# A selective-scan image kernel: two delta chunks begin earlier in the schedule, and a depthwise convolution's matmuls skip the zero rim

## The chip, the cores and the metric

One core of a Trainium2 chip runs the whole program. The metric is the device time in microseconds (us) of one execution. The kernel before takes 4227.16 us, the median of three runs (4224.71 to 4227.22).

The engines are called as in the profile: PE (TensorE), DVE (VectorE), ACT (ScalarE), POOL (GpSimd), and SP, which issues the DMAs.

## What is computed

Sixteen images of 256 channels by 32 x 32 pass through two blocks, each with a residual addition. Cut to what matters:

```python
# block 0: a depthwise 7x7 convolution whose filters are computed from the image itself
x = x + conv7x7_depthwise(groupnorm(x), filters(groupnorm(x)), padding=3)
# block 1: three levels (32x32, 16x16, 8x8) of a two-way state-space scan, 16 states
f1 = 1x1 conv; f2 = 2x2 stride-2 conv of f1; f3 = 2x2 stride-2 conv of f2
delta = softplus(dt @ x + bias);  B, C = rows of x @ xw
for n in range(16):                       # states
    h[t] = exp(delta[t] * A[n]) * h[t-1] + delta[t] * B[n,t] * x[t]
    y[t] += C[n,t] * h[t]
out = (layernorm(y) of all levels, upsampled and added) * silu(z)
x = x + 1x1 conv(out)
```

## The kernel before: how the work is tiled and ordered

**Three images are in work at once.** `stages` (L1425) runs a body for the images i, j = i+1 and m = i+2. Each body is 37 units, numbered k = 0 to 36, and then a bridge. The scans of image i run in the units; so do the convolution of j and the filters of m. The first two bodies have no image i: body one prepares image 0, body two convolves it and prepares image 1. Then 14 bodies run in a hardware loop and two follow it. Every engine has its own `unit` and `bridge` function, written out by hand, and semaphores tie them.

**Units.** Unit 0 is the 8x8 level, all 16 states in both directions. Units 1 to 4 are the 16x16 level, four states each, in both directions. Units 5 to 20 are the 32x32 level forward, a state each, and 21 to 36 the same backward. For one unit

- SP fetches the broadcast rows B and C (`get_b`, `get_c`, L367) for unit k+2 while unit k runs,
- ACT writes exp(delta * A) into the PSUM tensor `slot_b` (`decay`, L1173),
- POOL multiplies B with u = delta * x into `bx` (`inputs`, L1315 and L1318),
- DVE scans (L552) and multiplies with C (`weigh`, L561; for unit 0 these are L525 and L531), in halves of 512 columns,
- POOL adds the products over the states and into y (`gather`, L1338 and L1343), one unit behind.

**Chunks.** Delta and u are made in six chunks: 0 and 1 for the two small levels, 2 and 3 for the two halves of the forward and 4 and 5 for those of the backward 32x32 level. A chunk passes PE (`chunk`, L831 and L832), ACT (`chunk_exp`, L1124 to L1133), DVE (`chunk_first`, L500), ACT (`chunk_log`, L1139), DVE (`chunk_last`, L508 and L510) and POOL (`chunk_low`, L1285 and L1287). SP stores the B and C rows to DRAM (`put_rows`, L360), from where they are fetched broadcast. The tables `CHUNK_PE`, `CHUNK_FIRST` and `CHUNK_LAST` say in which unit each step stands; PE's and ACT's steps of chunks 2 and 3 stand in units 0 and 1, the rest in units 1 and 2. `CHUNKS_OF` says which unit needs which chunks: unit 5 needs 2 and 3, unit 21 needs 4 and 5.

**Convolution.** `taps` (L777) runs the 98 taps (two halves of the channels, 49 taps each) as matmuls with a diagonal stationary matrix over a zero-padded image `pad` of 38 x 38. A tap is 6 matmuls of 512 columns: three products of high and low 16-bit parts, times two halves of 16 rows. `BRIDGE_TAPS` and `ROOM` set how many taps stand in each bridge and unit, `HALF_AT` the unit where DVE adds the first channel half into `xn` (`conv_add`, L486), and `row_unit` the unit where ACT makes each row of diagonal matrices (`make_row`, L1059; four rows of buffers).

**Bridge.** Here the scans of i end: norms 4 and 5, the product with silu(z), the output projection (L857), DVE's last addition (`output`, L628), the store of `ob` (L411). In between, chunks 0 and 1 of j are made, `project_z` (L807) runs, and ACT ends with the first decays of j, `y_start` (L1153, the first value of y), `keep_x` (L1079, a copy of `xn` to `xc`), the rest of the diagonals and `copy_x` (L1086, `xr` to `xn`). SP loads the image after next into `xr` (L394) once `copy_x` is done.

```python
def stages(unit, bridge, eng):
    def body(i, j, m):
        for k in range(NU):
            unit(i, j, m, k)
        bridge(i, j, m)
BRIDGE_TAPS = (0, 1, 3, 3, 3, 3, 6, 9)
CHUNK_PE = {0: 2, 1: 3, 13: 4, 14: 5}
CHUNK_FIRST = {1: 2, 2: 3, 14: 4, 15: 5}
CHUNK_LAST = {1: 2, 2: 3, 15: 4, 16: 5}
```

## Time and profile before

| | |
|---|---|
| median of the runs | 4227.16 us |
| the profiled execution: its own time | 4222.54 us |
| its span, first to last instruction | 4220.7 us |
| PE busy | 3109.9 us (74%), 12620 matmuls |
| DVE busy | 3209.0 us (76%) |
| ACT busy | 2693.2 us (64%) |
| POOL busy | 3290.3 us (78%) |
| mean granted TensorE clock | 0.873 of full speed |

The profile gives one execution. Its views used here are the page (shares, the chain that ended last), the groups of instructions by line, the timeline of an engine (start, duration, line, and in brackets how long the engine sat idle before and what ended that), and the table of stretches. A steady body of the loop lasts about 249 us; the one shown runs from 2005 to 2254 us. Body two, with the convolution of image 0, lies between about 70 and 256 us.

### The profile page before, as it was taken

The page shows a single profiled execution, that of the slowest core. Times are in us where ns is not written, and L with a number is a line of the kernel's source. Part 1 is how long each engine was busy: PE and PEld are TensorE (multiplying, and loading weights), DVE is VectorE, ACT ScalarE, POOL GpSimd, SP SyncE. Part 2 cuts the span into 40 slices and gives each one's busy share as a digit, 9 for nine tenths or more (in the row PEclk, how much of TensorE's full clock was granted, in tenths as well). Part 3 has the DMA queues.
Part 4 walks back from the last instruction along what each step waited for, and adds up shares of the span by engine and source line. Part 5 has one row for each costly group of instructions (what it writes and reads, how often), then busy time and mean ns, then how long its engine had stood idle before and what let it go on. Part 6 is the DMA issues. An engine that isn't in the chain of part 4 may idle for free.

```text
span 4220.7 us, 53011 instructions
## 1 busy us (share of the span) xinstructions
PE 3109.9 (74%) x12620; PEld 1400.2 (33%) x12620; DVE 3209.0 (76%) x3975; ACT 2693.2 (64%) x6662; POOL 3290.3 (78%) x1908
## 2 busy tenths in 40 slices
PE   6978777887777788777777877788787778877511
PEld 3433333333333333333333433333333333333200
DVE  1058788787877878787887878788787887878877
ACT  4467766666766666666656766665677666666532
POOL 0059698796968969697896969889696987969797
PEclk8989888998888899889898988999898889988755
DMA  1025455453545545354553544445354554635544
GB/s 41 1 101 195 147 163 169 157 205 127 186 150 166 186 136 204 134 178 152 170 201 122 199 149 165 161 168 203 119 195 145 167 170 157 204 118 192 163 165 167
DMA packets 187275, 664.08 MB, mean 157 GB/s; under 512 B 22736, under 2 KB 24672, under 8 KB 186976
## 3 DMA queue, kind: packets, MB, share of 16 engines
q1 hardware_dynamic: 186976, 661.47, 46.4%
q14 instruction: 280, 2.29, 0.2%
q8 instruction: 19, 0.31, 0.0%
HBM read 639.76 MB, written 21.63 MB: 157 GB/s over the span
## 4 chain that ended last, share of the span: by engine, by line
POOL 28%; issue 19%; ACT 16%; PE 14%; DVE 13%; DMA 7%; POOLq 1%; DVEq 1%; SPq 0%; ACTq 0%
POOL bx L1315 13%; POOL y L1343 7%; DMA bb<-bc_rows 7%; ACT diag L1059 7%; PE pconv L790 6%; POOL h L1338 5%; DVE h L561 4%; DVE slot_c L552 2%; POOL bx L1318 2%; DVE rs L508 2%; ACT slot_b L1173 2%; PE pm L832 1%; PE pm L807 1%; PE pm L831 1%; DVE rs L500 1%
## 5 line engine op out<-in xcount | busy, mean ns | idle before, releaser
L790 PE MATMUL pconv<-pad,diag 128*128 128x512 f16 x9408 | 2270.5, 398 | 314.3 <-ACT diag L1059 210.0
L790 PEld LDWEIGHTS pconv<-pad,diag 128*128 128x128 f16 x9408 | 932.0, 100 | 1618.0 <-issue 346.0
L1343 POOL TENSOR_TENSOR y<-y,h 128x1024 f32<-128x1024 f32 (+2 forms) x672 | 1324.5, 1971 | 162.9 <-DVE h L561 139.6
L1173 ACT ACTIVATE slot_b<-delta,nega 128x512 f32<-128x512 f32 (+1 forms) x1280 | 805.4, 639 | 951.3 <-DVE slot_c L552 911.6
L1315 POOL TENSOR_TENSOR bx<-bb,u 128x1024 f32<-128x1024 f32 x512 | 1220.1, 2383 | 31.9 <-DMA bb<-bc_rows 31.9
L552 DVE TENSOR_TENSOR_SCAN slot_c<-slot_b,bx 128x512 f32<-128x512 f32 (+1 forms) x1024 | 954.4, 956 | 315.6 <-POOL bx L1315 214.6
L561 DVE TENSOR_TENSOR h<-slot_c,cb 128x512 f32<-128x512 f32 x1280 | 860.6, 674 | 35.9 <-POOL y L1343 35.9
L552 DVE TENSOR_TENSOR_SCAN slot_c<-slot_b,slot_c,bx 128x512 f32<-128x512 f32 x512 | 663.6, 1296 | 74.5 <-ACT slot_b L1173 18.2
L1059 ACT ACTIVATE diag<-id,chi 128x128 f16<-128x128 f16 x1568 | 498.1, 387 | 10.3 <-PE pconv L790 9.6
L1059 ACT ACTIVATE diag<-id,clo 128x128 f16<-128x128 f16 x1568 | 496.4, 386 | 0.0
L1338 POOL TENSOR_TENSOR h<-h 128x512 f32<-128x512 f32 (+3 forms) x384 | 349.9, 911 | 20.9 <-DVE h L531 3.4
L1285 POOL TENSOR_TENSOR delta<-delta,rs 128x512 f32<-128x512 f32 (+1 forms) x96 | 97.7, 1017 | 324.6 <-DVE rs L510 324.6
L1318 POOL TENSOR_TENSOR bx<-bb,u 128x1024 f32<-128x1024 f32 x64 | 158.8, 2482 | 125.5 <-DMA bb<-bc_rows 97.9
L500 DVE SCALAR_TENSOR_TENSOR rs<-qs,es 128x512 f32<-128x512 f32 (+1 forms) x96 | 64.9, 676 | 223.6 <-ACT qs L1133 223.6
L831 PE MATMUL pm<-f,wbc 128*32 128x512 f32 (+1 forms) x192 | 102.3, 620 | 147.0 <-ACT delta L1129 74.2
L1295 POOL TENSOR_TENSOR f<-f,lnw 128x98 f32<-128x98 f32 x16 | 6.2, 388 | 182.8 <-ACT f L1003 182.8
L1139 ACT ACTIVATE qs<-qs 128x512 f32<-128x512 f32 (+1 forms) x96 | 50.5, 526 | 153.7 <-DVE rs L500 153.7
L852 PE MATMUL pm<-es,ones 128*128 128x512 f32 (+1 forms) x128 | 62.7, 573 | 113.2 <-ACT es L1183 113.2
L846 PE MATMUL pm<-y,cen 128*128 128x512 f32 (+1 forms) x128 | 60.3, 554 | 89.2 <-POOL y L1343 40.6
L722 PE MATMUL pm<-ident,xh 128*128 128x128 f32 x256 | 47.0, 343 | 98.3 <-ACT xg L1094 72.1
L832 PE MATMUL pm<-f,wdelta 128*128 128x512 f32 (+1 forms) x192 | 116.9, 698 | 0.0
L695 PE MATMUL pconv<-sg,grp 128*128 128x8 f32 x32 | 9.5, 371 | 145.5 <-DVE sg L431 145.5
(171 smaller groups left out, 3095.9 us busy)
## 6 DMA issues: line engine op xcount, KB each, us to landing
bb<-bc_rows SPq DMA_DIRECT2D x592, 512.0 KB, 4.4
cb<-bc_rows SPq DMA_DIRECT2D x592, 512.0 KB, 4.4
xr<-in_x SPq DMA_DIRECT2D x16, 1024.0 KB, 5.0
out<-ob SPq DMA_DIRECT2D x16, 1024.0 KB
bc_rows<-rows SPq DMA_DIRECT2D x64, 64.0 KB, 1.6
w<-in_w SPq DMA_DIRECT2D x2, 256.0 KB
wc<-in_wc SPq DMA_DIRECT2D x2, 256.0 KB
bc_rows<-rows SPq DMA_DIRECT2D x16, 32.0 KB, 4.0
```

The lines of the kernel that those rows point to most:

```text
L500: nc.vector.scalar_tensor_tensor(er[:, k, 0:n], qs[:, k, 0:n], 1.0, es[:, k, 0:n], ALU.subtract, ALU.subtract).then_inc(ch_err.sem, 1)
L552: ins = nc.vector.tensor_tensor_scan(hv, av, bv, start, ALU.mult, ALU.add)
L561: nc.vector.tensor_tensor(half(h[:, q % HR], b), bank(slot_c, b), half(cb[:, k % CR], b), ALU.mult).then_inc(q_pr.sem, 1)
L790: ins = nc.tensor.matmul(bank(pconv, k), w, pad[:, t, part, rows:rows + 16, dx:dx + W], start=first and m == 0, stop=last and m == 2)
L831: nc.tensor.matmul(bank(pm, 0)[0:2 * NS, 0:n], wbc[:, st, :], f[:, fc:fc + n], start=True, stop=True).then_inc(ch_bc.sem, 1)
L832: nc.tensor.matmul(bank(pm, 1)[:, 0:n], wdelta[:, st, :], f[:, fc:fc + n], start=True, stop=True).then_inc(ch_dt.sem, 1)
L1059: ins = nc.scalar.activation(diag[:, r % RING, m, dx, :], id16[:, :], ACT.Copy, scale=(chi, clo)[m][:, t, dy * KK + dx:dy * KK + dx + 1])
L1173: ins = nc.scalar.activation(slot_b[:, o:o + w], delta[:, so + c:so + c + w], ACT.Exp, scale=nega[:, st, n0 + n:n0 + n + 1])
L1315: ins = pool.tensor_tensor(bx[:, k % 2, :], bb[:, k % BR, :], us, ALU.mult)
L1318: ins = pool.tensor_tensor(o, bb[:, k % BR, :].rearrange("p (m l) -> p m l", m=m), us[:, None, :].to_broadcast([P, m, ln]), ALU.mult)
L1338: pool.tensor_tensor(src[:, 0:m], src[:, 0:m], src[:, m:2 * m], ALU.add).then_inc(n_y.sem, 1)
L1343: pool.tensor_tensor(yv, yv, src[:, 0] if len(src.shape) == 3 else src, ALU.add).then_inc(q_y.sem, 1)
```

## The change

`chunk` 2 of the next image moves from unit 0 into the end of the bridge on PE, and its `chunk_exp` on ACT there too, ahead of `y_start`. Chunk 3's move from unit 1 to unit 0. DVE's `chunk_first` of chunks 2 and 3 moves from behind the unit's products to between them (`CHUNK_MID`). `keep_x` and `copy_x` move from the bridge to unit 1, and the load into `xr` from unit 0 to unit 2. On SP the stores of the rows come behind the two fetches of their unit. One bridge tap fewer is taken, which by the tables moves row 4 of the diagonals from the bridge to units 1 and 2, and `HALF_AT` from unit 10 to unit 11. `inside` cuts a tap's matmul to the pixels whose source lies in the image; the first product of a channel half and its last keep the full size. Over a channel half the cut leaves 212 x 212 of 224 x 224 columns, and 0.898 of all with the full-size ones.

```diff
--- before.py
+++ after.py
@@ -383,13 +383,12 @@
 
             def unit(i, j, m, k):
                 if i is not None:
-                    for c, v in CHUNK_PE.items():
-                        if k == c + 1:
-                            put_rows(i, v)
                     if k + 2 < NU:
                         get_b(i, k + 2)
                         get_c(i, k + 2)
-                if k == 0 and j is not None and m is not None:
+                    if k in ROWS_OUT:
+                        put_rows(i, ROWS_OUT[k])
+                if k == 2 and j is not None and m is not None:
                     sp.wait_ge(a_copy.sem, a_copy.at(m, 0))
                     sp.dma_start(xr[:, :, :], xv[m]).then_inc(x_in.sem, 16)
 
@@ -568,6 +567,8 @@
                     return
                 late = halves_of(k - 1)[-1] if k > 1 else None
                 for q, p in halves_of(k):
+                    if k in CHUNK_MID and (q, p) == halves_of(k)[2]:
+                        chunk_first(i, CHUNK_MID[k])
                     same = late is not None and banks(late[0])[late[1]] == banks(q)[p]
                     if same:
                         weigh(i, *late)
@@ -786,8 +787,10 @@
                     dh, dl = diag[:, r % RING, 0, dx, :], diag[:, r % RING, 1, dx, :]
                     for m, (w, part) in enumerate(((dh, 0), (dh, 1), (dl, 0))):
                         for k in range(2):
-                            rows = dy + 16 * k
-                            ins = nc.tensor.matmul(bank(pconv, k), w, pad[:, t, part, rows:rows + 16, dx:dx + W],
+                            whole = (first and m == 0) or (last and m == 2)
+                            r0, r1, c0, c1 = inside(dy, dx, k, whole)
+                            ins = nc.tensor.matmul(img(bank(pconv, k), W)[:, r0:r1, c0:c1], w,
+                                                   pad[:, t, part, 16 * k + r0 + dy:16 * k + r1 + dy, c0 + dx:c1 + dx],
                                                    start=first and m == 0, stop=last and m == 2)
                     if dx == KK - 1:
                         ins.then_inc(row_done.sem, 1)
@@ -885,6 +888,8 @@
                     output(i, 0)
                     output(i, 1)
                 some(6, 7)
+                if j is not None:
+                    chunk(j, 2)
 
             pre = {5: lambda m: sums1(m, sa, pm, a_sums, a_stats), 6: lambda m: sums2(m, sa, pm, a_sums, a_spread),
                    15: a_key_, 16: lambda m: (a_turn(m, 0), a_turn(m, 1)), 17: lambda m: (a_turn(m, 2), a_turn(m, 3)),
@@ -1221,14 +1226,11 @@
                         act.wait_ge(ob_ready.sem, ob_ready.at(j, 0))
                     decay(j, 1, 0)
                     decay(j, 1, 1)
-                    y_start(j)
-                    keep_x(j)
                 if m is not None:
                     make_row(m, RING - 1, KK)
-                    for r in range(RING, NR):
-                        if row_unit(r) == 0:
-                            make_row(m, r)
-                    copy_x(m)
+                if j is not None:
+                    chunk_exp(j, 2)
+                    y_start(j)
 
             pre = {6: a_mean_, 7: a_rstd_, 8: a_xh_, 16: a_keyb_, 17: lambda m: (a_xtc_(m, 0), a_xtc_(m, 1)),
                    18: lambda m: (a_xtc_(m, 2), a_xtc_(m, 3), a_exp_(m)),
@@ -1258,6 +1260,11 @@
                 if i is not None:
                     if k in CHUNK_PE:
                         chunk_exp(i, CHUNK_PE[k])
+                    if k == 1:
+                        keep_x(i)
+                if j is not None and k == 1:
+                    copy_x(j)
+                if i is not None:
                     if k == 5:
                         silu_exp(i)
                     if k == 6:
@@ -1374,13 +1381,15 @@
 
 TAPS = NR * KK
 PREP = NU - 4
-BRIDGE_TAPS = (0, 1, 3, 3, 3, 3, 6, 9)
+BRIDGE_TAPS = (0, 1, 3, 3, 3, 3, 6, 8)
 FIRST_TAPS = 2
 
 
 
-CHUNK_PE = {0: 2, 1: 3, 13: 4, 14: 5}
-CHUNK_FIRST = {1: 2, 2: 3, 14: 4, 15: 5}
+CHUNK_PE = {0: 3, 13: 4, 14: 5}
+ROWS_OUT = {0: 2, 1: 3, 14: 4, 15: 5}
+CHUNK_MID = {1: 2, 2: 3}
+CHUNK_FIRST = {14: 4, 15: 5}
 CHUNK_LAST = {1: 2, 2: 3, 15: 4, 16: 5}
 
 ROOM = [49 if k < 5 else 27 for k in range(NU)]
@@ -1396,6 +1405,14 @@
 
 
 HALF_AT = next(k for k in range(NU) if taps_at(k + 1) > TAPS // CT)
+
+
+def inside(dy, dx, k, whole):
+
+    if whole:
+        return 0, 16, 0, W
+    reach = KK // 2
+    return (max(reach - dy - 16 * k, 0), min(H + reach - dy - 16 * k, 16), max(reach - dx, 0), min(W + reach - dx, W))
 
 
 def row_unit(r):
```

**DVE, units 0 to 1 of the first body that scans** (`h` is the weighed product, `slot_c` the scan, `rs` the chunk's buffer er). Before:

```order
L561 TENSOR_TENSOR h<-slot_c,cb 128x512
L542 REGISTER_ALU
L552 SCALAR_TENSOR_TENSOR slot_c<-slot_b,bx 128x256 x2
L558 REGISTER_ALU
L560 ISA
L561 TENSOR_TENSOR h<-slot_c,cb 128x512
L497 ISA
L499 REGISTER_ALU
L500 SCALAR_TENSOR_TENSOR rs<-qs,es 128x512
L508 TENSOR_TENSOR rs<-qs,rs 128x512
L510 TENSOR_TENSOR rs<-rs,es 128x512
```

And now:

```order
L499 SCALAR_TENSOR_TENSOR rs<-qs,es 128x512
L541 ISA
L551 SCALAR_TENSOR_TENSOR slot_c<-slot_b,bx 128x256 x2
L557 REGISTER_ALU
L560 TENSOR_TENSOR h<-slot_c,cb 128x512
L541 REGISTER_ALU
L551 SCALAR_TENSOR_TENSOR slot_c<-slot_b,bx 128x256 x2
L557 REGISTER_ALU
L559 ISA
L560 TENSOR_TENSOR h<-slot_c,cb 128x512
L507 TENSOR_TENSOR rs<-qs,rs 128x512
L509 TENSOR_TENSOR rs<-rs,es 128x512
```

The first pass of chunk 2 (L500, now L499) has moved ahead of two of the unit's four scans; the last two passes stand where they stood.

**ACT, the end of the bridge** (`a` and `slot_b` are decays, `y` is `y_start`, `xc` is `keep_x`, `xn` is `copy_x`, `rows` begins a chunk). Before:

```order
L1173 ACTIVATE slot_b<-delta,nega 128x256 x4
L1153 ACTIVATE y<-f,vec 128x1024
L1153 ACTIVATE y<-f,vec 128x256
L1153 ACTIVATE y<-f,vec 128x64
L1153 ACTIVATE y<-f,vec 128x1280
L1153 ACTIVATE y<-f,vec 128x64
L1079 ACTIVATE xc<-xn 128x2048
L1059 ACTIVATE diag<-id,clo 128x128 x7
L1054 REGISTER_ALU
L1059 ACTIVATE diag<-id,chi 128x128 x7
L1059 ACTIVATE diag<-id,clo 128x128 x7
L1086 ACTIVATE xn<-xr 128x2048
```

And now:

```order
L1178 ACTIVATE slot_b<-delta,nega 128x256 x4
L1064 ACTIVATE diag<-id,clo 128x128 x7
L1126 REGISTER_ALU
L1128 ISA
L1129 ACTIVATE rows<-pm 32x512
L1133 ACTIVATE es<-pm,vec 128x512
L1134 ACTIVATE delta<-pm,vec 128x512
L1136 ACTIVATE es<-es 128x512
L1138 ACTIVATE qs<-es 128x512
L1158 ACTIVATE y<-f,vec 128x1024
```

Chunk 2 stands between seven diagonals and `y_start`; 14 diagonals and both copies have left the bridge.

**PE, units 13 and 14 of the loop** (`pm<-f` are the chunks 4 and 5, `pconv` the taps). Before:

```order
L825 REGISTER_ALU
L831 MATMUL pm<-f,wbc 32x512
L832 MATMUL pm<-f,wdelta 128x512
L790 MATMUL pconv<-pad,diag 128x512 x6
L777 REGISTER_ALU
L790 MATMUL pconv<-pad,diag 128x512 x6
L829 REGISTER_ALU
L831 MATMUL pm<-f,wbc 32x512
L832 MATMUL pm<-f,wdelta 128x512
```

And now:

```order
L828 REGISTER_ALU
L834 MATMUL pm<-f,wbc 32x512
L835 MATMUL pm<-f,wdelta 128x512
L792 MATMUL pconv<-pad,diag 128x13x29
L792 MATMUL pconv<-pad,diag 128x16x29
L792 MATMUL pconv<-pad,diag 128x13x29
L792 MATMUL pconv<-pad,diag 128x16x29
L792 MATMUL pconv<-pad,diag 128x13x29
L792 MATMUL pconv<-pad,diag 128x16x29
L832 REGISTER_ALU
L834 MATMUL pm<-f,wbc 32x512
L835 MATMUL pm<-f,wdelta 128x512
```

Between the two chunks stands one tap, where two stood.

## Rows read from the trace of the kernel before

**Rows 1.** The page: busy shares, and the chain that ended last

```profile
PE 3109.9 (74%) x12620; PEld 1400.2 (33%) x12620; DVE 3209.0 (76%) x3975; ACT 2693.2 (64%) x6662; POOL 3290.3 (78%) x1908
POOL 28%; issue 19%; ACT 16%; PE 14%; DVE 13%; DMA 7%; POOLq 1%; DVEq 1%; SPq 0%; ACTq 0%
```

**Rows 2.** Timeline of POOL, head of a body: start, us, operation [idle before]

```profile
2013.18 2.36 POOL L1318 TENSOR_TENSOR bx<-bb,u 128x1024 f32<-128x1024 f32 x1 [7.08 <-DMA bb<-bc_rows]
2015.49 2.94 POOL L1338 TENSOR_TENSOR h<-h 128x512 f32<-128x512 f32 x4
...
2021.88 0.32 POOL L1343 TENSOR_TENSOR y<-y,h 128x64 f32<-128x64 f32 x1 [0.16 <-POOL h L1338]
2025.58 1.27 POOL L1285 TENSOR_TENSOR delta<-delta,rs 128x512 f32<-128x512 f32 x1 [3.38 <-DVE rs L510]
...
2037.87 1.27 POOL L1285 TENSOR_TENSOR delta<-delta,rs 128x512 f32<-128x512 f32 x1 [0.69 <-DVE rs L510]
```

**Rows 3.** Timeline of DVE, the same stretch

```profile
2001.74 1.61 DVE L628 SCALAR_TENSOR_TENSOR ob<-slot_b,vec,xc 128x512 f32<-128x512 f32 x2 [1.72 <-PE slot_b L857]
...
2022.63 0.69 DVE L500 SCALAR_TENSOR_TENSOR rs<-qs,es 128x512 f32<-128x512 f32 x1 [2.96 <-ACT qs L1133]
2024.02 0.69 DVE L508 TENSOR_TENSOR rs<-qs,rs 128x512 f32<-128x512 f32 x1 [0.69 <-ACT qs L1139]
2024.74 0.69 DVE L510 TENSOR_TENSOR rs<-rs,es 128x512 f32<-128x512 f32 x1
...
2036.63 1.10 DVE L510 TENSOR_TENSOR rs<-rs,es 128x512 f32<-128x512 f32 x1
```

**Rows 4.** Timeline of ACT, the same stretch

```profile
2005.10 1.67 ACT L1173 ACTIVATE slot_b<-delta,nega 128x256 f32<-128x256 f32 x4 [2.74 <-DVE ob L628]
2006.71 3.27 ACT L1153 ACTIVATE y<-f,vec 128x1024 f32<-128x1024 f32 x5
...
2011.68 2.14 ACT L1059 ACTIVATE diag<-id,clo 128x128 f16<-128x128 f16 x7
...
2019.61 0.57 ACT L1124 ACTIVATE rows<-pm 32x512 f32<-32x512 f32 x1
...
2021.87 0.63 ACT L1133 ACTIVATE qs<-es 128x512 f32<-128x512 f32 x1
...
2053.82 0.69 ACT L1173 ACTIVATE slot_b<-delta,nega 128x512 f32<-128x512 f32 x1 [8.31 <-DVE slot_c L552]
```

**Rows 5.** Timeline of PE, bridge, end of the bridge and unit 1

```profile
1993.20 4.21 PE L790 MATMUL pconv<-pad,diag 128*128 128x512 f16 x18
...
2009.47 1.05 PE L831 MATMUL pm<-f,wbc 128*32 128x512 f32 x2
...
2021.47 1.88 PE L831 MATMUL pm<-f,wbc 128*32 128x512 f32 x2 [4.54 <-ACT delta L1129]
```

**Rows 6.** Timeline of DVE, units 14 to 16

```profile
2115.09 0.69 DVE L500 SCALAR_TENSOR_TENSOR rs<-qs,es 128x512 f32<-128x512 f32 x1 [1.16 <-ACT qs L1133]
...
2120.75 1.97 DVE L508 TENSOR_TENSOR rs<-qs,rs 128x512 f32<-128x512 f32 x1
2122.75 2.72 DVE L510 TENSOR_TENSOR rs<-rs,es 128x512 f32<-128x512 f32 x1
```

**Rows 7.** Timeline of POOL, units 14 and 15

```profile
2110.35 2.35 POOL L1315 TENSOR_TENSOR bx<-bb,u 128x1024 f32<-128x1024 f32 x1 [1.51 <-DMA bb<-bc_rows]
...
2117.25 1.27 POOL L1285 TENSOR_TENSOR delta<-delta,rs 128x512 f32<-128x512 f32 x1 [2.23 <-DVE rs L510]
```

**Rows 8.** Timeline of PE, units 10 to 14

```profile
2090.50 1.47 PE L790 MATMUL pconv<-pad,diag 128*128 128x512 f16 x6 [1.87 <-DVE xn L486]
...
2106.63 3.91 PE L790 MATMUL pconv<-pad,diag 128*128 128x512 f16 x12
```

**Rows 9.** Timeline of PE, body two

```profile
70.56 49.99 PE L790 MATMUL pconv<-pad,diag 128*128 128x512 f16 x216 [10.52 <-ACT diag L1059]
```

**Rows 10.** Timeline of DVE, body two

```profile
138.42 1.28 DVE L486 SCALAR_TENSOR_TENSOR xn<-pconv,csc,xn 128x1024 f32<-128x1024 f32 x1 [43.00 <-PE pconv L790]
```

## The prediction, made before the changed kernel ran

> **What bounds the kernel now.** I read the page first. No engine is busy all the time: POOL 78%, DVE 76%, PE 74%, ACT 64%, and the chain that ended last runs over POOL, ACT, PE and DVE in turn [rows 1]. So no single total sets the time. What counts is which wait ends last in each stage, and for that I went through the timelines of one steady body, 2005 to 2254 us, engine by engine.
>
> POOL works without a gap for most of a body. Its gaps lie at three places: the bridge, the head of the body, and units 14 to 16. In the head it waits 7.08 us for a transfer, then 3.38 us and 0.69 us for DVE's last pass of chunks 2 and 3 [rows 2]. DVE made chunk 2 late because its first pass waited 2.96 us for ACT and its second another 0.69 us [rows 3]. And ACT came to chunk 2 late, at 2019.61 us, since `y_start`, 21 diagonals and two copies stood ahead of it [rows 4]. PE had the chunk's first matmul issued at 2009.47 us [rows 5]. So in the head the bound is a queue on ACT, then the chain ACT, DVE, POOL.
>
> The convolution does not bound a steady body: DVE waits for it nowhere there, and where PE and the addition of the first channel half meet it is PE that waits, 1.87 us [rows 8]. It binds only in body two, where DVE sat idle 43.00 us until PE had done the first half of the taps [rows 10].
>
> **The head: chunks 2 and 3 start earlier.** On ACT, before, the decays began at 2005.10 us and took 1.67 us [rows 4]. Now seven diagonals of 2.14 us follow, then chunk 2, which took 2022.50 - 2019.61 = 2.89 us, so it is done at about 2011.7 us instead of 2022.5. DVE's first pass then waits for nothing. DVE's unit 1 still ends where it did (2019.68 us, 2022.63 less the wait of 2.96), plus the pass of 0.69 us, then two more passes of 0.69: 2021.7 us. POOL is through with the sums of unit 0 at 2021.88 + 0.32 = 2022.2 us [rows 2]. The wait of 3.38 us is gone, and so is the 0.69 us of chunk 3. Together 4.07 us.
>
> Against this, the passes now run while POOL works, where before POOL stood idle. A pass beside POOL took 1.10 us in unit 2 instead of 0.69 [rows 3]. The last two of chunk 2 lie on the path, so I take 0.8 us off: 3.25 us for each of 16 images, **52 us**. The bounds are 4.07 x 16 = 65 us, and 1.7 x 16 = 27 us where half is lost.
>
> What else moves there costs nothing, and this is the cover. The copies and 21 diagonals took ACT from 2009.98 to 2019.61 us; seven diagonals of 2.1 us stay, and 7.5 us go to units 1 and 2. ACT has room behind them: it later sat idle 8.31 us at once [rows 4]. Without that cover the decays of unit 3 would be late. On SP the load into `xr` now stands behind the fetches of unit 4 and a unit later; DVE reads `xr` at the end of unit 3, a further unit of 12 us on (chunk 2's step to chunk 3's, 2025.58 to 2037.87 us [rows 2]). The stores of rows 2 and 3 come behind two fetches but their sources are ready earlier, and no fetch but that of unit 5 waits for them. `y_start` is late next: it ends at 2011.7 + 3.27 = 2015.0 us, and POOL wants it at 2015.49 us [rows 2, 4]. The wait of 7.08 us for the transfer of unit 2 stays, since that fetch is issued behind the store of `ob`.
>
> **The bridge: three taps ahead of the output projection.** 18 matmuls take 4.21 us [rows 5], `project_z` and the output follow in PE's order, and DVE waits 1.72 us for the output [rows 3]. These taps keep 29 of 32 rows and 31 of 32 columns on average, 0.88, which saves 0.5 us. It shifts DVE's last addition, the store and all that follows. 15 bridges with both images: **7 us**; bounds 0 and 8.
>
> **Units 13 to 16: chunks 4 and 5.** Between chunk 4 and chunk 5 PE ran 12 tap matmuls in 3.91 us [rows 8], and one tap of the two is now behind chunk 5. That makes chunk 5 ready some 2 us earlier, and DVE's wait for it is 1.16 us [rows 6]; POOL's next step waits for DVE [rows 7]. So at most 1.16 us. The other way, the addition of the first channel half moves from unit 10 to 11, so PE meets it with a longer gap, and the spread of norm 1 comes behind two taps that may run at the lower clock. After a gap of 4.54 us the chunk's first matmul took 1.88 us instead of 1.05, nearly twice as long, as at the lower of the clock's two levels, 1.2 and 2.4 GHz [rows 5]. I take 1.0 us, 15 bodies: **15 us**; bounds 0 and 17.
>
> In unit 14 the fetch of B no longer stands behind the row store, so POOL's wait of 1.51 us for it goes [rows 7]. I cost it at nothing, as POOL waits for DVE 2.23 us a few steps later and simply waits longer; were that cover gone too, it would be worth up to 24 us.
>
> **Body two.** Its 588 tap matmuls take 49.99 / 216 = 0.231 us each [rows 9], 136 us, and PE is the bound there. Keeping 0.898 of the columns saves up to 13.9 us. Some of it is fixed cost per matmul: **13 us**; bounds 0 (if a matmul's time did not go by columns) and 14. In the 14 loop bodies the rest of the saving, about 13 us each, lies beside other work: PE waits for diagonals afterwards.
>
> **Sum.** 52 + 7 + 15 + 13 = 87 us. Against the profiled execution's own 4222.5 us that is 4135.5; the median of the runs stands 4.6 us above it, so I forecast **4140 us**, 2.1% faster.
>
> **The rivals.**
>
> *`y_start` is late.* The margin above is 0.5 us. It stands behind chunk 2 on ACT, and chunk 2 on PE stands behind DVE's clip of z. If PE's two matmuls take 1.88 us each, as at the lower clock [rows 5], ACT ends `y_start` at 2016.5 or later, and POOL's sums start 1 to 1.5 us later. 1.4 x 16 = 22 us less: 4162 us. For it: the margin. Against it: PE is busy right before. 18%.
>
> *The middle gives nothing.* PE meets the addition in unit 11 after a gap, its taps run at the lower clock, norm 1 and with it chunk 4 come later by what chunk 5 gains. 4155 us, or 4170 with a loss of 1 us per body. 12%.
>
> *The cut saves PE no time.* A matmul over rows of 29 to 31 pixels may take what a full one takes. Then the 7 and 13 us are not there: 4160 us. No row shows a trimmed matmul. 7%.
>
> *More is had:* the 1.51 us of unit 14 and the whole 4.07 us count. 87 + 24 + 13 = 124 us, 4103 us. 10%.
>
> *The other side: DVE's passes stretch beside POOL.* In unit 16 two passes next to POOL's long additions took 1.97 and 2.72 us instead of 0.69 [rows 6]. If all six passes of chunks 2 and 3 cost 2.72 us, that is 6 x 2.03 = 12.2 us more per body on DVE. The waits removed are 2.96 + 0.69 for chunk 2 [rows 3] and 0.69 for chunk 3 [rows 2], 4.3 us. The rest, 7.9 x 16 = 126 us, less the 35 us of the other terms, gives 4318 us. It decides once a pass costs on average more than 0.69 + 4.3 / 6 = 1.4 us. Against it: in the head POOL's operations are the short sums of units 0 to 2, four in 2.94 us [rows 2], and a pass beside them took 1.10 us [rows 3]. 5%.
> The Trainium skill (SBUF — State Buffer, the part on contention) speaks against the change here: a VectorE instruction with two SBUF inputs and a GpSimd instruction exclude each other for the whole instruction, and the loser is blocked. By that rule a pass would wait for the rest of whichever POOL operation runs, up to a whole addition; the rows of 2.72 us agree, and those of 1.10 us agree too, as the POOL operations there are short.
>
> *No change that can be measured.* The waits only move to POOL's next transfer or to the bridge. POOL has no gap between the head and unit 14, which speaks against it. 6%.
>
> **How the numbers follow.** The forecast has 42%, the rivals 18, 12, 7, 10, 5 and 6%. The range runs from the case with more to be had, 4100 us, to 4187 us, which takes in the late `y_start` together with an empty middle or with no saving from the cut; the bounds of the head alone give 4127 to 4165. It leaves out the slow side and no change. Within 0.2% of the time before, about what a measurement of this kernel can tell from no change, I put 6%; faster 0.88, slower 0.06.
>
> **What would show it.** In the profile after: POOL's waits for L510 in units 1 and 2 (3.38 and 0.69 us) near nothing, DVE's wait for ACT before its first pass of chunk 2 gone, that pass at about 1 us. `y_start` ending before POOL's first sum; if not, POOL's first L1338 shows a wait for ACT. Tap matmuls at about 0.21 us when dense. DVE's wait of 1.16 us in unit 15 gone. Body two shorter by 13 us, a loop body by 4 to 5 us out of 249. It would be wrong if POOL showed a new gap between units 3 and 13, or DVE passes in units 1 and 2 above 1.4 us.

## The result, and the profile after

| | before | after |
|---|---|---|
| median of the runs shown together | 4225.93 us (4 runs) | 4173.91 us (4 runs) |
| ratio, 95% interval | | 0.9879 [0.9864, 0.9895] |
| span of the profiled execution | 4220.7 us | 4171.0 us |
| first store of `ob` (bodies one to three) | at 506.17 us | at 495.31 us |
| mean of the 13 loop bodies that follow | 249.46 us | 246.71 us |
| last two bodies | 467.2 us | 464.1 us |

The change is 52 us faster, 1.2%, where 87 us were forecast. The spans differ by 49.7 us: 10.9 before the first store, 13 x 2.75 = 35.7 in the loop, 3.1 at the end.

First the busy times on the page of the kernel after, beside [rows 1], and two of its groups of instructions (busy, mean ns of one, then idle before them):

```profile
PE 2972.9 (71%) x12620; PEld 1412.1 (34%) x12620; DVE 3275.1 (79%) x3975; ACT 2698.8 (65%) x6662; POOL 3307.2 (79%) x1908
...
L1292 POOL TENSOR_TENSOR delta<-delta,rs 128x512 f32<-128x512 f32 (+1 forms) x96 | 97.6, 1017 | 272.0 <-DVE rs L509 272.0
L499 DVE SCALAR_TENSOR_TENSOR rs<-qs,es 128x512 f32<-128x512 f32 (+1 forms) x96 | 123.3, 1285 | 167.0 <-ACT qs L1138 167.0
```

The last of these groups in the kernel before:

```profile
L500 DVE SCALAR_TENSOR_TENSOR rs<-qs,es 128x512 f32<-128x512 f32 (+1 forms) x96 | 64.9, 676 | 223.6 <-ACT qs L1133 223.6
```

PE lost 137 us of work. DVE gained 66 us and POOL 17, though both do exactly what they did before. That is the first sign: something makes the same instructions longer. The first pass of a chunk (`chunk_first`, L499) takes 1285 ns in the mean where it took 676; that alone is 58 us of DVE's 66.

The head of a body, whose store of `ob` is at 1977.19 us. POOL's timeline after, beside [rows 2] (that body's store is at 2005.24 us):

```profile
1984.37 2.96 POOL L1325 TENSOR_TENSOR bx<-bb,u 128x1024 f32<-128x1024 f32 x1 [5.91 <-DMA bb<-bc_rows]
1987.30 3.27 POOL L1345 TENSOR_TENSOR h<-h 128x512 f32<-128x512 f32 x4
...
1990.92 3.61 POOL L1345 TENSOR_TENSOR h<-h 128x512 f32<-128x512 f32 x4
...
1994.98 1.27 POOL L1292 TENSOR_TENSOR delta<-delta,rs 128x512 f32<-128x512 f32 x1
...
2006.75 1.27 POOL L1292 TENSOR_TENSOR delta<-delta,rs 128x512 f32<-128x512 f32 x1
```

The low part of chunk 2 (L1292) no longer waits for DVE. It starts 17.8 us behind the store; before it was 20.3. That of chunk 3 has lost its wait of 0.69 us too. The head is now held by the landing of `bb` and POOL's own chain. That chain got longer: the sums of 2.94 us take 3.27 and 3.61, and `bx` 2.96 in place of 2.36.

ACT's timeline of the same head, beside [rows 4]:

```profile
1980.70 0.57 ACT L1129 ACTIVATE rows<-pm 32x512 f32<-32x512 f32 x1
...
1983.50 3.26 ACT L1158 ACTIVATE y<-f,vec 128x1024 f32<-128x1024 f32 x5
```

Chunk 2 is on ACT 3.5 us behind the store in place of 14.4. `y_start` ends at 1986.8, half a microsecond ahead of POOL's first sum.

Units 14 to 16, DVE's timeline, beside [rows 6]:

```profile
2078.01 2.55 DVE L499 SCALAR_TENSOR_TENSOR rs<-qs,es 128x512 f32<-128x512 f32 x1 [1.40 <-ACT qs L1138]
...
2084.20 1.14 DVE L499 SCALAR_TENSOR_TENSOR rs<-qs,es 128x512 f32<-128x512 f32 x1
2085.26 0.68 DVE L507 TENSOR_TENSOR rs<-qs,rs 128x512 f32<-128x512 f32 x1
2085.97 0.69 DVE L509 TENSOR_TENSOR rs<-rs,es 128x512 f32<-128x512 f32 x1
```

and POOL's, beside [rows 7]:

```profile
2077.64 2.37 POOL L1322 TENSOR_TENSOR bx<-bb,u 128x1024 f32<-128x1024 f32 x1
2082.44 2.35 POOL L1350 TENSOR_TENSOR y<-y,h 128x1024 f32<-128x1024 f32 x1 [2.43 <-DVE h L560]
2086.81 1.26 POOL L1292 TENSOR_TENSOR delta<-delta,rs 128x512 f32<-128x512 f32 x1 [2.02 <-DVE rs L509]
```

POOL's wait for the fetch, 1.51 us, is gone, as is DVE's 1.16 us ahead of chunk 5's pass. But chunk 4's first pass takes 2.55 us in place of 0.69.

Body two, the taps on PE and the addition of the first channel half on DVE, beside [rows 9, 10]:

```profile
70.68 46.77 PE L792 MATMUL pconv<-pad,diag 128*128 128x512 f16 x216 [10.52 <-ACT diag L1064]
```
```profile
133.65 1.28 DVE L485 SCALAR_TENSOR_TENSOR xn<-pconv,csc,xn 128x1024 f32<-128x1024 f32 x1 [40.34 <-PE pconv L792]
...
209.46 1.28 DVE L485 SCALAR_TENSOR_TENSOR xn<-pconv,csc,xn 128x1024 f32<-128x1024 f32 x1 [19.44 <-PE pconv L792]
```

A tap matmul takes 216.5 ns in the mean of this stretch where it took 231.4. In both kernels the granted clock is 0.50 until about 74 us, where the first ten or so matmuls lie. The rest run at the full clock, at about 211 ns after and 222 before. The second addition was at 219.09 us, so it comes 9.6 us earlier, not 13.

### The profile page after: what moved, and what is told of

It is laid out like the page before. It is cut to its first block, busy times and chain, and to the rows that moved or that the text cites. A ratio compares the mean times of both kernels' runs of the same rounds, so it can differ in the third digit from the quotient of the medians.

```text
span 4171.0 us, 53040 instructions
## 1 busy us (share of the span) xinstructions
PE 2972.9 (71%) x12620; PEld 1412.1 (34%) x12620; DVE 3275.1 (79%) x3975; ACT 2698.8 (65%) x6662; POOL 3307.2 (79%) x1908
## 4 chain that ended last, share of the span: by engine, by line
issue 21%; DVE 20%; POOL 19%; ACT 18%; PE 15%; DMA 6%; DVEq 1%; POOLq 0%; SPq 0%; ACTq 0%
ACT diag L1064 9%; POOL bx L1322 9%; PE pconv L792 8%; DVE h L560 7%; DVE slot_c L551 7%; POOL y L1350 6%; DMA bb<-bc_rows 6%; ACT slot_b L1178 3%; POOL h L1345 2%; DVE rs L507 1%; PE pm L810 1%; POOL bx L1325 1%; DVE xn L485 1%; PE pm L835 1%; PE pm L834 1%
## 5 line engine op out<-in xcount | busy, mean ns | idle before, releaser
L792 PE MATMUL pconv<-pad,diag 128*128 128x464 f16 (+11 forms) x9408 | 2142.0, 385 | 439.4 <-ACT diag L1064 304.1
L792 PEld LDWEIGHTS pconv<-pad,diag 128*128 128x128 f16 x9408 | 942.2, 102 | 1609.7 <-issue 362.8
L560 DVE TENSOR_TENSOR h<-slot_c,cb 128x512 f32<-128x512 f32 x1280 | 860.2, 673 | 23.7 <-POOL y L1350 23.7
L1345 POOL TENSOR_TENSOR h<-h 128x512 f32<-128x512 f32 (+3 forms) x384 | 365.9, 953 | 22.6 <-ACT y L1158 3.9
L1292 POOL TENSOR_TENSOR delta<-delta,rs 128x512 f32<-128x512 f32 (+1 forms) x96 | 97.6, 1017 | 272.0 <-DVE rs L509 272.0
L499 DVE SCALAR_TENSOR_TENSOR rs<-qs,es 128x512 f32<-128x512 f32 (+1 forms) x96 | 123.3, 1285 | 167.0 <-ACT qs L1138 167.0
L849 PE MATMUL pm<-y,cen 128*128 128x512 f32 (+1 forms) x128 | 70.4, 636 | 123.6 <-POOL y L1350 49.1
L723 PE MATMUL pm<-ident,xh 128*128 128x128 f32 x256 | 56.9, 396 | 137.8 <-ACT xg L1099 70.4
L834 PE MATMUL pm<-f,wbc 128*32 128x512 f32 (+1 forms) x192 | 84.0, 520 | 37.4 <-ACT delta L1134 19.9
L1294 POOL TENSOR_TENSOR u<-delta,f 128x512 f32<-128x512 f32 (+1 forms) x96 | 97.8, 1018 | 7.5
L723 PEld LDWEIGHTS pm<-ident,xh 128*128 128x128 f32 x256 | 45.1, 204 | 155.6 <-ACT xg L1099 80.2
```

Source lines behind the costliest of these rows:

```text
L499: nc.vector.scalar_tensor_tensor(er[:, k, 0:n], qs[:, k, 0:n], 1.0, es[:, k, 0:n], ALU.subtract, ALU.subtract).then_inc(ch_err.sem, 1)
L560: nc.vector.tensor_tensor(half(h[:, q % HR], b), bank(slot_c, b), half(cb[:, k % CR], b), ALU.mult).then_inc(q_pr.sem, 1)
L723: ins = nc.tensor.transpose(bank(pm, g % 2)[:, (2 * b + t) * P:(2 * b + t + 1) * P], xh[:, t, n * P:(n + 1) * P], ident[:, :])
L792: ins = nc.tensor.matmul(img(bank(pconv, k), W)[:, r0:r1, c0:c1], w, pad[:, t, part, 16 * k + r0 + dy:16 * k + r1 + dy, c0 + dx:c1 + dx], ...
L834: nc.tensor.matmul(bank(pm, 0)[0:2 * NS, 0:n], wbc[:, st, :], f[:, fc:fc + n], start=True, stop=True).then_inc(ch_bc.sem, 1)
L1345: pool.tensor_tensor(src[:, 0:m], src[:, 0:m], src[:, m:2 * m], ALU.add).then_inc(n_y.sem, 1)
```

## Landmarks for the experiments

The same four points of a body tell where each kernel gains. They are starts on POOL, in us behind the store of `ob` that opens the body, as means over the twelve middle bodies: the low parts of chunks 2, 3 and 4, and the low half of the weights (`wlo`); then the next store. Three more columns count bodies of those twelve. "Held" bodies have chunk 2's low part 0.9 us or more later than the kernel's best body; they are split by what is seen in them. In those held by products, DVE's two products of unit 0 take 4.4 to 4.5 us instead of 2.33. In those held by `bb`, the products take 2.33 us and POOL's `bx` behind them starts only 8.3 us or more behind the store, when `bb` has landed. "Slow PE" has the two centring matmul groups of the bridge at 1.3 to 2.0 us instead of 1.08 and 1.02.

| kernel | chunk 2 | chunk 3 | chunk 4 | `wlo` | next store | held by products | held by `bb` | slow PE |
|---|---|---|---|---|---|---|---|---|
| before | 20.34 | 32.63 | 112.60 | 175.24 | 249.44 | 0 | 0 | 1 |
| after | 18.17 | 29.95 | 110.01 | 172.64 | 246.54 | 4 | 0 | 2 |
| e1 no cut | 17.61 | 29.40 | 109.50 | 172.18 | 246.65 | 0 | 0 | 3 |
| e2 cut only | 20.34 | 32.62 | 111.77 | 174.61 | 248.37 | 0 | 0 | 1 |
| e3 store first | 18.33 | 30.12 | 109.50 | 172.15 | 245.80 | 1 | 4 | 0 |
| e4 half at 10 | 17.84 | 29.62 | 109.68 | 172.30 | 246.06 | 0 | 0 | 1 |
| e5 first passes behind | 18.33 | 30.64 | 110.70 | 173.31 | 247.65 | 3 | 1 | 5 |
| e6 rows only | 17.93 | 29.70 | 109.75 | 172.36 | 246.34 | 2 | 0 | 2 |
| e7 columns only | 17.65 | 29.43 | 109.51 | 172.14 | 246.28 | 0 | 1 | 1 |
| e8 store and turn | 17.87 | 29.65 | 107.84 | 170.79 | 245.79 | 1 | 0 | 10 |
| e9 bridge tap | 19.68 | 31.46 | 110.36 | 173.32 | 245.70 | 8 | 0 | 0 |
| e10 turn, no cut | 17.71 | 29.49 | 108.87 | 171.83 | 246.04 | 0 | 1 | 1 |
| e11 changed again | 18.37 | 30.15 | 110.20 | 172.83 | 246.60 | 2 | 3 | 1 |
| e12 POOL waits | 20.27 | 32.05 | 110.45 | 173.40 | 245.77 | 0 | 0 | 0 |

From chunk 3 to chunk 4 the kernel before took 79.97 us, the one after 80.06: the middle lost a tenth where 1.0 us was forecast to be gained. From `wlo` to the next store it was 74.20 and is 73.90. In bodies without slow PE matmuls it is 74.05 us before, 74.07 in e1 and 73.62 after; a slow body takes 1.6 us more.

## The experiments

All twelve kernels compute the whole result. They were run in groups of four (e1 to e4), four (e5 to e8), three (e9 to e11) and one (e12), each beside the kernel before on the same chip, whose medians there were 4219.2, 4223.8, 4223.0 and 4222.3 us. So ratios are compared, and times within a group.

**The two halves of the change.** e1 is the change without the cut:

```
-                            whole = (first and m == 0) or (last and m == 2)
+                            whole = True
```

> The changed kernel with every tap's matmul at its full 512 columns (same result, no cut). Theory: the cut is worth 10 us in body two and 0.45 us per bridge (15 bridges, 7 us), and nothing elsewhere, as PE waits for diagonals or DVE in a steady body. Expected 4174 + 17 = 4191 us (4186 to 4196); a loop body 0.5 us longer than the 246.7 us of the changed kernel. Rival: the cut takes cover away in the middle of a body (PE meets the addition of the first half after a gap, at the lower clock), so that without it a loop body is shorter: 4165 to 4180 us.

Measured: 4179.7 us, ratio 0.9901 [0.9886, 0.9916]. By the ratios that is 9 us above the changed kernel, not the 17 expected, and a loop body is 0.1 us longer, not 0.5. The rival's range holds the time, but its shorter loop body isn't there. e2 puts the cut alone into the kernel before.

> The kernel before with the cut alone. Theory: 10 us in body two and 7 us in the bridges, nothing else: 4226 - 17 = 4209 us (4203 to 4214), a loop body of 249.0 us against 249.5. Rival: the taps between chunks 4 and 5 lie on the path too (two taps, 0.4 us per body), then 4202 us.

Measured: 4200.97 us, ratio 0.9953 [0.9939, 0.9966]. In the changed order the cut is worth about 10 us ahead of the first store (505.22 against 495.31 us) and nothing in a loop body (246.65 against 246.54 us). That nothing is a difference: the stretch from `wlo` to the next store is 0.6 us shorter, and chunk 2's low part comes 0.6 us later behind the store (17.61 against 18.17). In the old order the cut is worth 1.1 us a body, where 0.5 was expected: chunk 4 comes 0.8 us earlier by it, as the rival had it, and the stretch behind `wlo` is 0.4 us shorter. So in the loop the two parts don't add up. By the ratios the order alone is worth 42 us and the cut alone 20, together 51 to 56 (e11); with intervals of 6 us each way those totals alone would not show it.

**The middle.** e3 restores the old place of the store of rows in SP's order for units 14 and 15:

```
+                    if k in ROWS_OUT and k > 1:
+                        put_rows(i, ROWS_OUT[k])
                     if k + 2 < NU:
                         get_b(i, k + 2)
                         get_c(i, k + 2)
-                    if k in ROWS_OUT:
+                    if k in ROWS_OUT and k < 2:
                         put_rows(i, ROWS_OUT[k])
```

> The changed kernel with SP's stores of chunk rows 4 and 5 again ahead of the two fetches of units 14 and 15; those of chunks 2 and 3 stay behind. Theory: the wait of POOL for that fetch (1.51 us before, 0 after) was cover. With it POOL stands idle while DVE makes its first pass of chunk 4, which took 0.69 us before and 2.55 us after, beside a POOL operation of 2.37 us. With the store first again: POOL waits about 1.5 us for the fetch, the pass takes 0.7 us, the last step of chunk 4 on POOL comes 1.8 us earlier, a loop body is about 245.0 us, and the kernel 4174 - 27 = 4147 us (4140 to 4155). Rival: the middle lost time since the addition of the first half moved to unit 11 (PE at the lower clock there); then this changes nothing or costs the 1.5 us: 4172 to 4197 us.

Measured: 4158.3 us, ratio 0.9852 [0.9836, 0.9867]; the next store at 245.80 us, chunk 3 to chunk 4 in 79.38 us. The gain is less than half of the 27 us expected, but the rival's "nothing" falls. DVE's timeline of units 14 and 15, and POOL's:

```profile
2070.14 0.69 DVE L501 SCALAR_TENSOR_TENSOR rs<-qs,es 128x512 f32<-128x512 f32 x1 [1.32 <-ACT qs L1140]
...
2074.63 2.48 DVE L501 SCALAR_TENSOR_TENSOR rs<-qs,es 128x512 f32<-128x512 f32 x1
```
```profile
2071.89 2.36 POOL L1324 TENSOR_TENSOR bx<-bb,u 128x1024 f32<-128x1024 f32 x1 [1.95 <-DMA bb<-bc_rows]
2074.21 2.35 POOL L1352 TENSOR_TENSOR y<-y,h 128x1024 f32<-128x1024 f32 x1
```

With POOL made to wait 1.95 us for its fetch again, chunk 4's pass falls into that gap and takes 0.69 us. The next pass, 1.14 us after the change, now meets POOL's `y` and ends at 2077.1 us, half a microsecond behind it. So 1.9 us were gained and 1.3 lost, and the low part of chunk 4 comes 0.7 us earlier from chunk 3 on. The kernel before shows what the wait had been worth, DVE and POOL:

```profile
2109.35 0.69 DVE L500 SCALAR_TENSOR_TENSOR rs<-qs,es 128x512 f32<-128x512 f32 x1 [1.14 <-ACT qs L1133]
```
```profile
2106.44 2.40 POOL L1343 TENSOR_TENSOR y<-y,h 128x1024 f32<-128x1024 f32 x1
2110.35 2.35 POOL L1315 TENSOR_TENSOR bx<-bb,u 128x1024 f32<-128x1024 f32 x1 [1.51 <-DMA bb<-bc_rows]
```

There the same pass lay between two of POOL's operations. After the change it starts at 2078.01 us while POOL is at work until 2080.01, and ends at 2080.56, as if it had begun only when POOL was through. So does e3's second pass.
The Trainium skill (SBUF — State Buffer, the part on contention) states this: a VectorE instruction with two SBUF inputs and a GpSimd instruction that reads SBUF exclude each other for a whole instruction. The trace agrees, and also where an instruction doesn't have two such inputs: DVE's product L560, one of whose inputs is in PSUM, keeps 673 ns in the mean over 1280 of them in the kernel after, though POOL is busy 79% of the time.

e4 tests the rival, that the addition of the first channel half costs the middle its gain by having moved from unit 10 to 11:

```
-HALF_AT = next(k for k in range(NU) if taps_at(k + 1) > TAPS // CT)
+HALF_AT = 10
```

> The changed kernel with DVE's addition of the first channel half back in unit 10. Theory (the pass beside POOL): no effect within 0.2%, 4166 to 4182 us, as ACT waited only 1.05 us for the spread of norm 1 and DVE did not wait for norm 1. Rival (the addition in unit 11 is what cost the middle its gain): 1 to 1.8 us less per body, 4147 to 4160 us.

Measured: 4165.3 us, ratio 0.9872 [0.9857, 0.9888], from chunk 3 to 4 in 80.06 us as after. No effect on the middle. The mean body is 0.5 us shorter, but that lies in the head, where none of the twelve bodies happened to be held.

**The head.** e5 puts the first passes of chunks 2 and 3 behind the products again:

```
-CHUNK_MID = {1: 2, 2: 3}
-CHUNK_FIRST = {14: 4, 15: 5}
+CHUNK_MID = {}
+CHUNK_FIRST = {1: 2, 2: 3, 14: 4, 15: 5}
```

> The changed kernel, but VectorE's first passes of chunks 2 and 3 stand behind the products of units 1 and 2 again instead of between them; everything else as changed. Theory A (placement matters a little: in the changed kernel the head is now held by POOL's own chain from the landing of bb, 2.96 + 3.27 + 3.61 us, so a later pass first eats slack of about 0.5 us and then costs): low part of chunk 2 starts 0.3 to 1.5 us later behind the out store than the changed kernel's 18.01 us, chunk 3 likewise, time 4178 to 4200 us (ratio to the kernel before 0.989 to 0.994). Rival B (the placement is most of the head's gain, 2.3 us a body): chunk 2's low part back at 20 us or more, time 4208 to 4215 us. Rival C (the pass between the products only stretches POOL's sums, 3.27 and 3.61 us against 2.94 before, so that behind them is better): low part at 17.0 to 17.5 us, time 4160 to 4170 us.

Measured: 4188.2 us, ratio 0.9912 [0.9899, 0.9926]. In bodies that aren't held chunk 2's low part is at 17.7 to 17.9 us as after, and chunk 3's at 30.0 to 30.2 against 29.5 to 29.8, since DVE's second pass waits 0.70 us for ACT again. In bodies held by the products chunk 2's low part is 1.9 us late, where after the change it is 1.0. B and C fall. Theory A's time and cost hold, but not its place: chunk 2 in a body that isn't held comes no later. The passes between the products bring 0.3 to 0.4%, part of it by the clock in the bridge (slow in five of twelve bodies of e5). Most of the head's gain is ACT's order, which e5 has too.

**The cut.** e6 leaves out rows only, e7 columns only. By symmetry each leaves out 12 of 224 lines of the seven shifts, the same number of columns of PE's work.

```
-    return (max(reach - dy - 16 * k, 0), min(H + reach - dy - 16 * k, 16), max(reach - dx, 0), min(W + reach - dx, W))
+    return max(reach - dy - 16 * k, 0), min(H + reach - dy - 16 * k, 16), 0, W
```

> The changed kernel, with the tap products cut only in whole image rows (all 32 columns kept). Mean columns per matmul 485 of 512. Theory A (columns cost 0.417 ns each at the full clock, and what the full cut loses, about 5 ns per matmul, is the broken rows of 29 to 31 columns): the tap matmul in body two takes 231 - 11 = 220 ns, body two is 6 us shorter than with no cut (full cut: 9.6), ratio to the kernel before 0.9886. Rival B (the 5 ns are a fixed cost of any matmul on a window that is not the whole bank): 225 ns, 3 us shorter, ratio 0.9893.

> The changed kernel, with the tap products cut only in columns (all 16 rows kept, rows of 29 to 32). Mean columns per matmul again 485 of 512. Theory A (broken rows cost about 5 ns more): the tap matmul in body two takes 225 to 226 ns, body two 3 to 3.5 us shorter than with no cut, ratio 0.9893. Rival B (fixed cost for any cut window): the same 225 ns as with rows alone. Rival C (no extra cost of either alone): 220 ns both, and the two savings would then add up to more than the full cut's 15 ns.

The first stretch of taps in body two, of e1, e6 and e7 in turn:

```profile
70.39 49.96 PE L792 MATMUL pconv<-pad,diag 128*128 128x512 f16 x216 [10.52 <-ACT diag L1064]
```
```profile
67.93 48.34 PE L792 MATMUL pconv<-pad,diag 128*128 128x512 f16 x216 [10.52 <-ACT diag L1064]
```
```profile
70.91 49.01 PE L792 MATMUL pconv<-pad,diag 128*128 128x512 f16 x216 [10.52 <-ACT diag L1064]
```

| | ns per matmul, first stretch | from the first tap to the second addition, us | saved, us |
|---|---|---|---|
| nothing cut (e1) | 231.3 | 148.51 | |
| rows only (e6) | 223.8 | 142.22 | 6.29 |
| columns only (e7) | 226.9 | 145.61 | 2.90 |
| both (after) | 216.5 | 138.78 | 9.73 |

Rows save twice what columns save, for the same number of columns streamed. Per matmul of all 588 that is 10.7 and 4.9 ns. The rates of the first stretch show less of a difference, since its 36 of 49 taps hold only 51 of the 84 lines that the row cut leaves out. An estimate of what there was to save: each of the two leaves out 15,744 columns, which at the 222 ns that 512 columns take at the full clock are worth 6.8 us. Rows save nearly that, columns less than half. The totals, 4170.7 us, 0.9873 [0.9857, 0.9888] and 4172.6 us, 0.9879 [0.9864, 0.9894], can't be told from the change's own, as expected of 3 to 7 us. Theory A holds in the trace, and rival B, that rows and columns save alike, falls: a matmul whose rows are broken to 29 to 31 pixels costs more than its columns. Why it does wasn't taken apart.

**On from e3.** e8 also turns the order in unit 15, so that chunk 4's last passes go ahead of chunk 5's first:

```
+                    if k in CHUNK_LAST:
+                        chunk_last(i, CHUNK_LAST[k])
                     if k in CHUNK_FIRST:
                         chunk_first(i, CHUNK_FIRST[k])
-                    if k in CHUNK_LAST:
-                        chunk_last(i, CHUNK_LAST[k])
```

> The changed kernel with two edits for the middle: the store of rows goes out ahead of the fetches in units 14 and 15 (as in e3_store_first), and in unit 15 VectorE does the two last passes of chunk 4 ahead of the first pass of chunk 5. Theory A (a VectorE pass that meets a POOL operation on SBUF lasts until that operation ends): one pass, the first of the last two of chunk 4, still meets POOL's y of 2.35 us and takes about 2.5 us, the other 0.69; POOL's low part of chunk 4 starts about 0.7 us earlier than in e3_store_first (which had it at 109.72 us behind the out store), chunk 5's first pass then meets POOL's low part of chunk 4 and takes 1 to 1.5 us; time 4145 to 4160 us, ratio 0.982 to 0.986. Rival B (what chunk 4 gains, chunk 5 gives back, since its logarithm comes later): chunk 4's low part 0.7 us earlier, chunk 5's at 118.08 us as in e3, time 4156 to 4162 us, ratio 0.985 to 0.9865.

Measured: 4158.0 us, ratio 0.9843 [0.983, 0.9857]. Both expected ranges hold that time. Chunk 4 does come 1.7 us earlier than in e3, 107.84 us, and chunk 5 some 1.3 us earlier, so rival B falls; `wlo` is 1.4 us earlier; and the next store is where it was, 245.79 against 245.80. The gain went in the bridge. PE's timeline there and the granted clock (table of stretches: length, busy PE, PE's loads, DVE, ACT, POOL, then the clock), e8:

```profile
2198.09 1.65 PE L851 MATMUL slot_b<-y,cen 128*128 128x512 f32 x2
2199.53 1.91 PE L851 MATMUL slot_c<-y,cen 128*128 128x512 f32 x2
```
```profile
2185.00:2190.00 5.00, 5.00 (x10) 1.98 (x9) 3.40 (x4) 5.00 (x16) 2.04 (x2) 0.68 0.00 0
2190.00:2195.00 5.00, 3.92 (x19) 2.33 (x18) 0.89 (x2) 5.00 (x16) 2.73 (x2) 1.00 0.00 0
2195.00:2200.00 5.00, 3.91 (x17) 2.30 (x16) 0.23 (x1) 2.70 (x11) 0.00 (x0) 0.85 0.01 2
2200.00:2205.00 5.00, 5.00 (x13) 1.63 (x12) 0.45 (x2) 3.57 (x9) 2.10 (x3) 0.81 0.61 216
```

and e3:

```profile
2198.59 1.08 PE L851 MATMUL slot_b<-y,cen 128*128 128x512 f32 x2
2199.50 1.02 PE L851 MATMUL slot_c<-y,cen 128*128 128x512 f32 x2
```
```profile
2195.00:2200.00 5.00, 3.91 (x21) 2.42 (x19) 0.23 (x1) 3.23 (x12) 0.00 (x0) 1.00 0.01 2
2200.00:2205.00 5.00, 5.00 (x19) 2.17 (x18) 0.85 (x3) 4.57 (x11) 1.65 (x3) 1.00 0.62 216
```

In e8 the clock falls from the upper level, 2.4 GHz, to the lower, 1.2, for part of these stretches, after PE had come back to the upper one by 2190. Ahead of all this PE had idled 4.96 us, in e3 as in e8. Ten of twelve bodies show it, and those are 1.6 us longer between `wlo` and the store. e9 puts one tap more into the bridge, between the two projections, where PE idled 1.08 us:

```
-BRIDGE_TAPS = (0, 1, 3, 3, 3, 3, 6, 8)
+BRIDGE_TAPS = (0, 1, 3, 4, 4, 4, 6, 8)
```

> e8_store_and_turn, with one tap more (6 products) in the bridge between the projection onto f and its lower levels, where TensorE idled 1.1 us in e8 (2.2 us in e3), and one tap less behind. Why: in e8 ten of the twelve middle bodies show the two centring matmuls of the bridge at 1.41 to 1.79 and 1.91 us, in e3 none does (1.08 and 1.02 us), and each of the ten is 1.6 us longer between the start of the low half of the weights and the next out store; the granted clock of the 5 us around them is 0.81 to 0.85 in e8 and 1.00 in e3. Theory A (the clock fell after the idle stretches around the projection, and a filled one keeps it): centring matmuls at 1.08 and 1.02 us in most bodies, mean body 244.2 to 244.8 us, time 4135 to 4145 us, ratio 0.9795 to 0.982. Rival B (the fall depends on where the stage lies, not on this gap): nothing changes in the matmuls, the tap delays the lower levels by 0.2 to 0.5 us, mean body 246 us, time 4156 to 4165 us, ratio 0.984 to 0.9865.

Measured: 4152.8 us, ratio 0.9833 [0.982, 0.9846]. e10 is e8 with nothing cut:

> e8_store_and_turn with all tap products whole (nothing cut). Theory A (the shorter tap products leave TensorE more idle, so its clock falls more often in the bridge, and the cut takes there what it gives elsewhere): fewer than 5 of 12 bodies with slow centring matmuls against 10 of 12 in e8, mean body 244.5 to 245.3 us, body two and its neighbours 9 to 10 us longer, time 4148 to 4158 us. Rival B (the fall comes from the stage being earlier, whatever the taps take): 8 or more of 12 bodies with slow ones, mean body 245.8 us or more, time 4165 to 4172 us, ratio 0.9865 to 0.988.

Measured: 4176.3 us, ratio 0.9892 [0.9877, 0.9907], a mean body of 246.0 us. Both take the falls away (0 and 1 of 12). In both PE has more work ahead of that place than in e8. But e3 kept the clock with more idle time there (2.22 us), so the gap alone doesn't decide, and what does stays open. Neither reached the time expected of it. In e10 whole taps bring chunk 4 a microsecond later than in e8. In e9 `wlo` to the next store is 72.4 us in place of 75.0, but the next head takes back 1.8, for a reason given below.

**What holds the head.** e11 is the changed kernel again, in one group with e9 and e10.

> The changed kernel as it is, beside the two others on one chip, to set the variants' gains against it. Both theories: ratio 0.988 (0.9864 to 0.9895 before). Theory A (VectorE's second product of unit 0 and POOL's first bx of the body block each other whenever bx starts ahead of it): again some of the twelve middle bodies, 3 to 7, show POOL's low part of chunk 2 at 18.8 to 19.0 us behind the out store and the product at twice its length (4.50 against 2.33 us for two), and the rest 17.8 us; a body is 1.0 to 1.2 us longer for it. Rival B (that difference is one of the DMA's landing alone): products at 2.33 us in both kinds of body.

Measured: 4169.7 us, ratio 0.9868 [0.9853, 0.9883]; five of twelve bodies held. In two of the five the products take 4.5 us, as theory A has it. In the other three they take 2.33 us, and `bx` starts only 8.7 to 9.2 us behind the store, as rival B has it. So there are two ways to be held, and neither theory covers both. In the first profile after, all four held bodies are of the first kind; in e3 four of five are of the second. Why `bb` lands later in some bodies wasn't looked into.

The first kind. Two bodies of the first profile after, DVE's timeline, the one held first:

```profile
2968.36 4.50 DVE L530 TENSOR_TENSOR h<-cb,h 128x1024 f32<-128x1024 f32 x2
...
3215.17 2.33 DVE L530 TENSOR_TENSOR h<-cb,h 128x1024 f32<-128x1024 f32 x2
```

and POOL's:

```profile
2969.18 2.59 POOL L1325 TENSOR_TENSOR bx<-bb,u 128x1024 f32<-128x1024 f32 x1 [5.14 <-DMA bb<-bc_rows]
...
3216.49 3.23 POOL L1325 TENSOR_TENSOR bx<-bb,u 128x1024 f32<-128x1024 f32 x1 [5.64 <-DMA bb<-bc_rows]
```

In the first, `bb` lands 0.8 us into the products of the least level (L530). POOL's `bx` goes ahead of the second product, which ends only after it: 4.50 us for two. In the second, `bx` starts 1.3 us into them and is itself the one that stands, 3.23 us for 2.36. What decides is whether `bx` or the second product starts first. Here that is a few tenths of a microsecond of a transfer's landing, 6.7 or 6.9 us behind the store, and the held body is 1.0 to 1.2 us longer. Here it is the body in which `bb` lands earlier that is held.

Why the kernel before has no such body among the twelve, though `bb` lands as early there: its second product starts 6.49 us behind the store, and `bx` never ahead of 6.57. After the change the second product starts at 6.68 to 6.97. The scan ahead of it became longer, and it is the cut that did this, not the order. POOL's `bx` of unit 1 and DVE's scan of unit 0, in e1 (store at 1986.39 us) and after (1977.19 us):

```profile
1984.96 2.36 POOL L1325 TENSOR_TENSOR bx<-bb,u 128x1024 f32<-128x1024 f32 x1 [2.13 <-issue]
1987.32 4.53 DVE L524 TENSOR_TENSOR_SCAN h<-a,b 128x1040 f32<-128x1040 f32 x2
```
```profile
1976.11 2.35 POOL L1325 TENSOR_TENSOR bx<-bb,u 128x1024 f32<-128x1024 f32 x1 [2.04 <-issue]
1978.12 4.74 DVE L524 TENSOR_TENSOR_SCAN h<-a,b 128x1040 f32<-128x1040 f32 x2
```

The cut brings the store forward by 0.45 us, but this `bx` hardly comes forward with it. It ended as the scan began, 0.93 us behind the store; now it ends 0.3 us into the scan, and the scan loses 0.2 us, in other bodies up to 0.47. With nothing cut (e1, e10) the scan takes 4.53 us and no body is held by the products. With the cut in the old order (e2) the second product takes 3.4 us in five of the twelve bodies, at no cost, since chunk 2 waits for ACT there. In e9, whose bridge is shorter still, `bx` of unit 1 lies wholly beside the scan, which takes 5.9 to 6.1 us, and eight bodies are held: that is the 1.8 us.

e12 makes POOL wait, in e9:

```
+                    if k == 0:
+                        pool.wait_ge(q_pr.sem, q_pr.at(i, 2))
                     if k + 1 < NU:
                         inputs(i, k + 1)
```

> e9_bridge_tap with one wait more: in unit 0 POOL holds its first operation (bx of unit 1) until VectorE has done both products of the least level. Why: in e9 eight or nine of the twelve middle bodies show those two products at 4.44 us and POOL's bx starting at 6.69 us behind the out store, between them; the low part of chunk 2 is then at 20.0 us, and in the other bodies, where bx starts at 8.6 us, the products take 2.33 us and the low part is at 19.0 us. Theory A (the second product stands until bx has ended, since both use SBUF alone): with the wait the products take 2.33 us in all bodies, bx starts at about 9.2 us, the low part is at 19.1 to 19.3 us, a body is 0.7 us shorter in the mean (245.0 us), time 4138 to 4146 us, ratio 0.980 to 0.982. Rival B (the products are long for another reason, the traffic of the DMA that brings bb say): they stay at 4.4 us in most bodies, bx comes at 11.3 us and the low part at 21 us, a body is 1 us longer, time 4162 to 4172 us, ratio 0.985 to 0.988.

Measured: 4156.5 us, ratio 0.9846 [0.9832, 0.9859]. DVE and POOL, one body whose store is at 1717.74 us:

```profile
1718.67 4.53 DVE L526 TENSOR_TENSOR_SCAN h<-a,b 128x1040 f32<-128x1040 f32 x2
1723.12 2.33 DVE L532 TENSOR_TENSOR h<-cb,h 128x1024 f32<-128x1024 f32 x2
```
```profile
1725.70 4.67 POOL L1327 TENSOR_TENSOR bx<-bb,u 128x1024 f32<-128x1024 f32 x2 [9.83 <-DVE h L532]
```

The products take 2.33 us in every body and no body is held, which bears out theory A's cause for the first kind. Its gain isn't there, by a slip of mine: the expectation took the operation at 6.69 us for the first of unit 0, but that is `bx` of unit 2. The wait stands ahead of `bx` of unit 1, which in e9 starts 0.2 us behind the store, beside the scan L526 (5.9 to 6.1 us there, 4.53 here). It is held too, both run in a row afterwards, and chunk 2's low part is at 20.27 us. A wait ahead of the later `bx` wasn't tried.

**The best version** is e9: 4152.8 us against 4169.7 of the changed kernel in the same group and 4223.0 of the kernel before. Its interval lies below those of both. It can't be told from e3, e8 and e12, whose intervals overlap its own.

## Why the prediction was right and wrong

Direction and range were right; the sum of 87 us was 35 too high, near to the rival of 4170 us.

- **Head**, 3.25 us a body: right for the order alone. In e1 chunk 3's low part comes at 29.40 us, 3.23 ahead of 32.63. The 0.8 us taken off for passes beside POOL is included there, though in the profile after what pays it is POOL's own sums, 1.0 us longer, rather than the passes (1.15, 0.87 and 0.78 us). With the cut the mean is 2.68: 43 us in place of 52. The step that failed is the bridge's "It shifts DVE's last addition, the store and all that follows". POOL's `bx` of unit 1 hardly shifts, so the scan of unit 0 meets it, and a third of the bodies is then held by the products. What the cut gives in a bridge, 0.45 us, it takes back in the head, 0.56 in the mean.
- **`y_start`** ended 0.5 us ahead of POOL's first sum, by the margin of the text. In the held body at 2969 us POOL waits 0.48 us for it, as `bb` lands earlier.
- **Bridge**, 0.5 us a body: right, 0.45 where the clock doesn't fall; 0.3 in the mean, with one body of twelve more at the lower clock than before.
- **Middle**, 1.0 us a body: nothing. The failed step is the fetch of unit 14, costed at nothing. The wait of 1.51 us was the only time that POOL stood still about chunk 4's first pass: at 2109.35 us it took 0.69 us, between POOL's operations that ended at 2108.8 and began at 2110.35. With the wait gone the pass takes 2.55. DVE's wait of 1.16 us ahead of chunk 5's pass did go, as forecast, but that pass takes 1.14 us for 0.69. The text had the rule for it and priced it in the head alone. The rival "the middle gives nothing" named the right outcome, near 4170 us, by the wrong mechanism (e4).
- **Body two**, 13 us: 9.6 to 9.7. The saving per matmul is 16.5 ns over all 588 where 22 were had in mind; most of the missing part is the cost of rows with 29 to 31 pixels (e6, e7). Dense taps at the full clock do take 0.21 us.
- **The loop bodies get nothing more from the cut**: right after the change (e1), where even the bridge's part is lost again, wrong in the old order (e2), where it was 1.1 us a body.
- **The other side**, six passes of 2.72 us: only one of the six in the head is long (2.51 us, chunk 3's first). The six take 1.24 us on average; the point from which it decides, 1.4 us, was not reached.

## What to carry to other kernels

Before a wait is taken off one of two engines that exclude each other, look at what the other does in that gap: the gap may be the only place where its instruction runs at full speed, and then the wait only changes its name. Price such a move with every two-input SBUF operation of VectorE laid against every GpSimd operation, for both may be the one that stands. The same holds where a step becomes shorter: what was behind a GpSimd operation may now begin beside it. And when a stage becomes shorter and the body doesn't, look at TensorE's granted clock in the next stage that PE decides.

## What was not expected of the hardware

- After the change one body's time has two values, 1.0 to 1.2 us apart, by which of two instructions starts first, `bx` at 6.7 or at 6.9 us behind the store. A late landing of `bb`, at 8.7 us or later, costs about as much.
- Leaving out columns inside each row saved 2.90 us, leaving out as many columns in whole rows 6.29.
- With chunk 4 served 1.7 us earlier, the clock in the bridge fell in ten of twelve bodies instead of none, and took back the whole gain.
